# Sum of squares of a normalised group: eight transposes and two additions over rows in place of eight products with a column of ones

## The reference

```python
yg = y * jax.nn.silu(gate)
yg_g = yg.reshape(Bsz, S, NG, GROUP)
rstd = jax.lax.rsqrt(jnp.mean(jnp.square(yg_g), axis=-1, keepdims=True) + EPS)
out = (yg_g * rstd).reshape(Bsz, S, INTER) * norm_w
return out @ out_proj_w.T
```

## Time and profile before

| | us |
|---|---|
| median of 3 runs | 2133.59 |
| lowest and highest run | 2131.73, 2133.9 |
| profiled execution, its own time | 2129.18 |
| profiled execution, span | 2127.4 |
| PE busy | 2087.6 (98%) |
| DVE busy | 1641.0 (77%) |
| ACT busy | 1432.5 (67%) |
| POOL busy | 1053.0 (49%) |

### The profile page before, as it was taken

One profiled execution on the slowest core, in us unless ns is written; L12 is line 12 of the kernel. 1 busy time (PEld: TensorE's weight loads), 2 busy tenths in 40 slices (PEclk: granted clock), 3 DMA queues, 4 the chain that ended last, 5 costly groups with the idle time before them and its releaser, 6 DMA issues.

```text
span 2127.4 us, 34908 instructions
## 1 busy us (share of the span) xinstructions
PE 2087.6 (98%) x12642; PEld 1736.3 (82%) x12652; DVE 1641.0 (77%) x2661; ACT 1432.5 (67%) x3090; POOL 1053.0 (49%) x758
## 2 busy tenths in 40 slices
PE   8999999999999999999999999999999999999999
PEld 7866698887788888888888888888888888888887
DVE  7777773325889898898898989889889898998222
ACT  5498743335978777778777877767877787784332
POOL 5577545451355356354455535634445553555452
PEclk9999999999999999999999999999999999999999
DMA  3000013332343233233223323323322432331332
GB/s 139 1 1 2 1 61 94 95 90 77 131 139 134 72 113 125 74 129 139 90 90 139 134 76 109 127 75 126 139 90 90 139 134 75 110 114 58 96 95 84
DMA packets 65337, 202.53 MB, mean 95 GB/s; under 512 B 7056, under 2 KB 9104, under 8 KB 56976
## 3 DMA queue, kind: packets, MB, share of 16 engines
q1 hardware_dynamic: 65168, 200.31, 27.8%
HBM read 197.39 MB, written 2.88 MB: 94 GB/s over the span
## 4 chain that ended last, share of the span: by engine, by line
PE 91%; DVE 4%; ACT 3%; issue 1%; POOL 0%; DMA 0%; DVEq 0%; SPq 0%; ACTq 0%; POOLq 0%
PE ps L1808 86%; PE ps L2206 3%; PE ps L1993 2%; PE ps L1823 1%; ACT eb L960 0%; DVE bst L1186 0%; DVE x L1590 0%; ACT xTh L688 0%; DVE xTl L1209 0%; ACT pr_a L827 0%; DVE eb L1560 0%; DVE PT L1416 0%; DVE rs L1361 0%; ACT pr_b L827 0%; DMA cst<-cst_in 0%
## 5 line engine op out<-in xcount | busy, mean ns | idle before, releaser
L579 POOL TENSOR_TENSOR wAl<-rawA,wAh 128x512 fp32r<-128x512 f32 x233 | 341.6, 1481 | 364.4 <-ACT wAh L721 363.9
L1808 PE MATMUL ps<-xTh,wAh 128*128 128x512 f32 (+1 forms) x1528 | 419.4, 396 | 4.7 <-DVE xTl L1209 4.7
L1808 PE MATMUL ps<-xTl,wAh 128*128 128x512 f32 (+1 forms) x1528 | 405.9, 387 | 0.0
L1808 PE MATMUL ps<-xTh,wAl 128*128 128x512 f32 (+1 forms) x1528 | 405.2, 387 | 0.0
L1514 DVE SCALAR_TENSOR_TENSOR work<-ps,chp,work 128x510 f32<-128x510 f32 (+2 forms) x465 | 343.2, 743 | 22.7 <-ACT work L923 12.7
L1808 PEld LDWEIGHTS ps<-xTl,wAh 128*128 128x128 f32 x1528 | 285.5, 188 | 60.2
L1808 PEld LDWEIGHTS ps<-xTh,wAl 128*128 128x128 f32 x1528 | 285.2, 188 | 58.4
L1808 PEld LDWEIGHTS ps<-xTh,wAh 128*128 128x128 f32 x1528 | 277.3, 188 | 67.6 <-issue 12.8
L585 POOL TENSOR_TENSOR wBl<-rawB,wBh 128x512 fp32r<-128x512 f32 x108 | 139.8, 1308 | 388.7 <-ACT wBh L725 388.7
L960 ACT ACTIVATE eb<-eb,gc 128x128 f32<-128x128 f32 x1008 | 307.6, 392 | 0.0
L923 ACT ACTIVATE work<-ps,gpar 128x512 f32<-128x512 f32 x155 | 119.4, 771 | 128.8 <-PE ps L1808 96.9
(11 more groups left out here) (210 smaller groups left out, 3960.4 us busy)
## 6 DMA issues: line engine op xcount, KB each, us to landing
eb<-scr_decays SPq DMA_DIRECT2D x62, 1536.0 KB, 6.4
rawA<-ma_in SPq DMA_DIRECT2D x144, 256.0 KB, 6.8
rawA<-fa_in SPq DMA_DIRECT2D x88, 256.0 KB, 2.6
rawB<-mb_in SPq DMA_DIRECT2D x64, 256.0 KB, 2.8
rawB<-fb_in SPq DMA_DIRECT2D x44, 256.0 KB, 2.6
x<-x_in SPq DMA_DIRECT2D x8, 256.0 KB, 6.7
x_out<-x SPq DMA_DIRECT2D x8, 256.0 KB, 2.4
wqraw<-wqkv_in SPq DMA_DIRECT2D x1, 1536.0 KB, 11.1
```

What stands on the lines that cost most here:

```text
L579: nc.gpsimd.tensor_tensor(wAl[:, slot, :], rawA[:, slot, :], wAh[:, slot, :].bitcast(F32), ALU.subtract).then_inc(A_lo, 1)
L1808: return nc.tensor.matmul(o, l, r, start=start, stop=end, **kw)
```

## The change

The 8 products of a group with a column of ones become 8 transposes of the 128 x 128 tiles of `sq`, four in bank 4 and four in bank 7. The second four wait for the evacuation of tile t = 6, which frees bank 7. Each four raise the semaphore `m_ss` by one, so the counts that others wait for double. VectorE then adds over each row of 128 channels, in one reduction for each bank (128 x 4 x 128 to 128 x 4), and then scales. `out_products` of v = 1 waits for `mean_square` already at tile t = 0 (bank 7), beside its wait at t = 2 (bank 4), which stays.

```diff
+    SQBANK = (4, 7)
...
             if v == 0:
-                pool.wait_ge(m_ss, g + FREE)
+                pool.wait_ge(m_ss, 2 * g + FREE)
...
-        def mean_square(g, bank):
-            dve.wait_ge(m_ss, g + 1 + FREE)
-            nc.vector.tensor_scalar(ss[:, :], ps[:, bank, 0:NT], 1.0 / GROUP, EPS, ALU.mult,
+        def mean_square(g):
+            for p in range(2):
+                dve.wait_ge(m_ss, 2 * g + p + 1 + FREE)
+                last = nc.vector.tensor_reduce(ss[:, 4 * p:4 * p + 4],
+                                               ps[:, SQBANK[p], :].rearrange("p (t c) -> p t c", t=4), AX.X, ALU.add)
+            link(last)
+            nc.vector.tensor_scalar(ss[:, :], ss[:, :], 1.0 / GROUP, EPS, ALU.mult,
                                     ALU.add).then_inc(m_var, 1)
...
                 if t == 0:
+                    if v == 1:
+                        pe.wait_ge(m_var, g + FREE)
                     pe.wait_ge(m_osum, 32 * g + 8 * j - 1 + FREE)
...
-        def sum_squares(g, bank):
+        def square_transposes(g):
             pe.wait_ge(m_sq, 2 * TPG * (g + 1) + FREE)
-            pe.wait_ge(m_osum, 32 * g + 24 + 6 + FREE)
             for t in range(NT):
-                last = mm(ps[:, bank, t:t + 1], sq[:, t * P:(t + 1) * P], ones, True, True)
-            last.then_inc(m_ss, 1)
+                if t % 4 == 0:
+                    pe.wait_ge(m_osum, 32 * g + 24 + 6 + t // 4 + FREE)
+                last = nc.tensor.transpose(ps[:, SQBANK[t // 4], (t % 4) * P:(t % 4 + 1) * P], sq[:, t * P:(t + 1) * P],
+                                           ident)
+                if t % 4 == 3:
+                    last.then_inc(m_ss, 1)
```

More of the change, by code:

```diff
@@ L1605, in evacuate @@
                                         ALU.add).then_inc(m_osum, 1)
-        def mean_square(g, bank):
-            dve.wait_ge(m_ss, g + 1 + FREE)
-            nc.vector.tensor_scalar(ss[:, :], ps[:, bank, 0:NT], 1.0 / GROUP, EPS, ALU.mult,
+        def mean_square(g):
[5 more added lines that the diff above has]
+            nc.vector.tensor_scalar(ss[:, :], ss[:, :], 1.0 / GROUP, EPS, ALU.mult,
                                     ALU.add).then_inc(m_var, 1)
         def last_mean_square(p):
-            dve.wait_ge(m_ss, NG + p + FREE)
+            dve.wait_ge(m_ss, 2 * (NG - 1) + p + 1 + FREE)
             nc.vector.tensor_scalar(ss[:, 4 * p:4 * p + 4], ps[:, SBANK[p], 0:4], 1.0 / GROUP, EPS, ALU.mult,
@@ L1671, in step @@
                 if v == 0:
-                    mean_square(g - 1, 4)
+                    mean_square(g - 1)
             ending = last and v == TPG - 2
@@ L2268, in step @@
                 if v == 0:
-                    sum_squares(gp, 4)
+                    square_transposes(gp)
             y_products(v, g, 0)
```

## The result

The changed kernel takes 2123.67 us, median of 5 runs (2122.93 to 2124.62). The kernel before took 2133.9 beside it (5 runs, 2131.73 to 2135.14). The ratio is 0.9949, 95% interval 0.9938 to 0.996: faster by 10.2 us, 0.5%. The forecast was 2127.4 with a range from 2125.0, so the sign was right, the gain was 1.6 times the forecast 6.2 us, and the time lies outside the range.

What follows compares the result with a forecast made beforehand. PE was taken to bound the state-space loop. Per group 1.83 - 0.87 - 0.05 - 0.03 = 0.88 us, seven times 6.2 us; profiled 2129.18 became 2123.0, and with 4.4 added the median 2127.4, range 2125.0 to 2131.5.

Steps and rivals of the forecast that it cites:

- What bounds the kernel: State-space loop: PE busy for all 177.07 us of a group, so a microsecond off PE is one off the kernel.
- PE, what goes: Burst of 8 products with ones: 1.77 us plus 0.06 for the passage behind it, together 1.83 us per group.
- The 0.06 added for the passage: First batch for y behind the burst takes 0.71 us, the next 0.65; the difference was counted as saved.
- PE, what comes: Eight transposes in place of the burst: 0.87 us per group with the passage behind them, 0.109 each.
- The two unseen terms: Per group, 0.05 us for passage to products of half the columns, 0.03 for the fifth transpose's wait on tile 6's evacuation.
- DVE: Two reductions and a scaling, 1.34 us of new work, hide in 2.29 us idle; 0.14 left before `skip`.
- Rival C: At the burst: transposes of `sq` leave two passes each, 1.77 us for eight, saving nothing; 2133.6 us, chance 0.04.
- D: Behind each of 7 bursts the array's clock falls to its lower level; 10.6 us more, 2144, chance 0.04.
- How the numbers follow: Whole kernel: profiled execution 2129.18 less 6.2 is 2123.0 us; the median lies 4.4 higher, so 2127.4.
- "Cost 0" for POOL: POOL's power ends at about 725.61, hundredths later; nothing of PE's is queued behind it, so cost 0.

Runs made afterwards that it cites:

- e5: The kernel before with two added GpSimd waits, so VectorE comes first at both contested places; 2128.54 us, against 2129.69 for the kernel before beside it.
- e6: The changed kernel with two added GpSimd waits, so VectorE comes first at both contested places; 2122.88 us.
- e8: As e5, but each burst of 8 products with ones is run twice; 2150.35 us.
- e9: As e6, but each burst of 8 transposes is run four times over; 2141.5 us.
- e16: e5 once more on another chip; 2129.21 us, against 2136.77 for the kernel before beside it.
- e3: The changed kernel with one added wait: GpSimd waits for VectorE's products of eb before the low parts of wA; 2124.08 us.
- e11: As e6, but in place of each reduction VectorE copies one column for each tile; 2122.71 us.
- e10: As e6, but each of a group's two reductions is done twice and linked to the next operation; 2131.63 us.
- e7: The changed kernel again, unchanged, on the chip of e5 and e6; 2123.77 us, against 2129.69 for the kernel before.

## Why the prediction was wrong

**What bounds the kernel:** right. The stretches of e5, e6, e8, e9 and e16 have PE busy for the whole of them, and each change of PE's time showed in the total. Left out was the one data wait that did leave PE idle, 0.64 us in the fifth stretch: the text names only the wait that recurs.

**PE, what goes:** 1.77 for the burst was right; e8's repetition of it took 1.79 more. The 0.06 added for the passage behind it was not, since it stays behind the transposes too (0.71 to the second batch for y, then 0.65, in both kernels).

**PE, what comes:** 0.87 was right (0.109 each in e9). The two unseen terms were mis-sized. The fifth transpose didn't wait at all, for 0.03 (8 records in 1.03 us, no gap). The passage to the products of half the array's columns, taken at 0.05, measured 0.96 - 0.87 = 0.09. So the products for y come 1.77 - 0.96 = 0.81 us earlier, and the group is 0.77 to 0.78 shorter; the last 0.04 are given back further on, and no run says by what. That is 5.4 us instead of 6.2 for seven; e5 less e6 gives 5.7. The two traces differ by 6.1, close to the forecast 6.2, by luck: 5.4, and 0.85 for the one late group of before, and 0.27 in the time ahead of the first burst, less 0.5 that the changed kernel's trace lost again in the tail, where its clock fell (e3's tail, without that, is 0.5 shorter).

**DVE:** right. Idle time ahead of `skip` was forecast at 0.14 and is 0.25; e11 shows the work hidden, and e10 the edge, with another wait of PE behind it than the prediction named.

**Rival C** is out (56 records for 56 transposes), and **D** as well: granted clock 1.00 in all stretches, and e9.

**The step that failed** stands under "How the numbers follow": "The median of the runs lies 4.4 higher, at 2133.59, so the predicted median is 2127.4." It took the 4.4 us between the trace and the median for something that both kernels carry. They belonged to the kernel before: in its five traces GpSimd took the contested place behind 17 of 35 bursts, for 0.85 us each, and the profiled execution was a lucky one with 1 of 7. The changed kernel has VectorE first in 14 of 14, so its trace (2123.11) and its median (2123.67) agree, and the change gained those losses beside its own 5.4 to 5.7 us. On e7's chip, where the two waits took only 1.2 off the kernel before, it gained 5.9, near the forecast 6.2. How the 4.4 us of the result's own chip divide between late groups and the clock in the tail is not shown, as no execution with that median was traced. The other half of the failure is "Cost 0" for POOL: it asked who waits for POOL's results, not whom POOL holds up. The fifth stretch of before, 177.92, with PE's wait for `eb`, was there to be read, and would have shown the mechanism, though not how often it strikes.

Still open is why the changed kernel has the luckier order. What the traces do show is a count. GpSimd's recorded start is ahead of VectorE's at the contested place every time: by 62 to 80 ns in the five traces of before, by 44 to 54 ns and once 69 in the two of the changed kernel. Over all 49 places, VectorE came first in all 23 with a lead of 72 ns or less, and in 9 of the 26 with 73 ns or more. The change brings VectorE's products 0.81 us nearer to the burst and GpSimd's operation 0.78, which shortens the lead by 0.03. That fits, but no run moved a start by so little on purpose. Nor was a lower clock in the tail tested by itself; it is worth up to 2 us in either kernel.

The best version run is e6, the changed kernel with both orders fixed, 2122.88 us against 2123.77 for the changed kernel on the same chip; their runs overlap. For the kernel before the two waits by themselves brought 7.6 us on one chip; on another it was 1.2, which is not clear of the noise (ratio 0.9996, 0.9987 to 1.0005).

## What to carry to other kernels

When the profiled execution and the median of runs differ by more than the effect that is looked for, look in the trace for a group that repeats with one member out of line: what cost it there may be what costs the typical run, and a change that moves the phase by a hair can take it away or bring it on. Where GpSimd and VectorE start on SBUF operands within a tenth of a microsecond of each other, and one of them feeds the critical engine, try an order by a wait; here it cost nothing (stretches of 176.3 in e6 as without it). Do it at all such places at once: with one fixed, the next one showed up. A product with a column of ones cost two passes in fp32 here (0.22 us), a transpose one (0.11), and the adding that is left can go to VectorE while it has idle time exactly there.

## What the runs showed of the hardware

- Where GpSimd's subtraction and VectorE's two products, all with two SBUF operands, started within 0.08 us of each other, either VectorE's pair took 1.1 us longer (3.44 instead of 2.34), or GpSimd's one operation 2.3 longer (3.57 instead of 1.30). Which came first changed from group to group and from chip to chip in one and the same program, and the recorded starts have GpSimd ahead in both cases.
- The same contention at a second place left PE idle for 2.4 us in five groups. Three times the lower clock followed for about 3.5 us, and the group lost 4.1 to 4.3 us instead of 2.7.
- Bursts of one-column fp32 products 3.5 us long were followed by TensorE's lower clock in 5 of 7 cases, though the engine was busy without a gap; bursts of fp32 transposes of the same length in none of 7.
- An fp32 product leaves two records and takes 0.22 us with 128 x 128 weights even for one column; an fp32 transpose leaves one and takes 0.109.
